# Expert layer of a four-stage kernel: blocks scatter their results to token rows, plain loads bring them back

## The reference

```
router = xf @ gate_w.T
probs = softmax(router);  top_p, top_i = top_k(probs, 2)
h = silu(xf @ expert_fc1[e].T) * (xf @ expert_fc2[e].T)      # for each expert e
out_e = h @ expert_proj[e].T
y = sum over the token's two experts of top_p * out_e
y = y + sigmoid(xf @ shared_gate_w.T) * shared(xf)
x = x + y
```

## Time and profile before

| what | value |
|---|---|
| device time, median of 3 runs (lowest to highest) | 869.14 us (868.95 to 869.23) |
| the profiled execution's own time | 869.01 us |
| its span, from the first to the last instruction | 867.2 us |
| mean granted TensorE clock (share of full speed) | 0.988 |
| PE busy, instructions | 813.6 us, 4543 matmuls |
| DVE, ACT, POOL busy | 456.9, 318.4, 161.9 us |
| transfers | 72.07 MB, mean 83 GB/s |

### The profile page before, as it was taken

The page is one execution under the profiler, slowest core; times in us unless marked ns, Lnnn a source line. Parts: engine busy times, 40 slices in busy tenths (PEclk is TensorE's granted clock), DMA queues, the critical chain, the costliest instruction groups (busy, mean ns, idle before and its releaser), DMA issues.

```text
span 867.2 us, 12754 instructions
## 1 busy us (share of the span) xinstructions
PE 813.6 (94%) x4543; PEld 568.6 (66%) x4543; DVE 456.9 (53%) x1054; ACT 318.4 (37%) x651; POOL 161.9 (19%) x256
## 2 busy tenths in 40 slices
PE   6979799889899977999999999998999999999998
PEld 3567566666567765677777776776766655555567
DVE  5999766757422225866464666476543252322223
ACT  3987777555033322443323243332312211111111
POOL 3652744113500070111111111111100000000000
PEclk9998999999999997999999999999999999999999
DMA  4002860281253230023010100100224344354431
GB/s 139 2 2 40 264 231 2 52 224 55 98 173 107 74 91 12 19 61 92 25 37 25 37 25 27 35 25 25 63 79 128 112 129 125 122 148 131 130 107 48
DMA packets 63957, 72.07 MB, mean 83 GB/s; under 512 B 14200, under 2 KB 48504, under 8 KB 63896
## 3 DMA queue, kind: packets, MB, share of 16 engines
q1 hardware_dynamic: 59048, 64.06, 24.8%
q0 software_dynamic: 1536, 4.20, 1.5%
q10 hardware_dynamic: 3312, 3.02, 1.0%
HBM read 55.45 MB, written 14.75 MB: 81 GB/s over the span
## 4 chain that ended last, share of the span: by engine, by line
PE 76%; DVE 10%; issue 5%; ACT 5%; another core or an unknown queue 1%; SPq 1%; DMA 1%; POOL 1%; DVEq 0%; ACTq 0%; POOLq 0%
PE bank L930 10%; PE bank L892 10%; PE bank L906 10%; PE bank L1107 8%; PE bank L1074 8%; PE bank L969 6%; PE bank L955 6%; PE bank L636 3%; PE bank L1857 3%; PE bank L658 2%; PE bank L1814 2%; PE bank L1841 2%; ACT arena L1914 1%; PE bank L979 1%; DVE sh L2395 1%
## 5 line engine op out<-in xcount | busy, mean ns | idle before, releaser
L1139 ACT ACTIVATE arena<-bank 128x512 f32<-128x512 f32 (+1 forms) x64 | 34.7, 544 | 230.0 <-PE bank L892 194.4
L1247 DVE TENSOR_TENSOR arena<-arena,bank 128x512 f32<-128x512 f32 (+1 forms) x47 | 30.7, 654 | 151.7 <-PE bank L906 151.7
L930 PE MATMUL bank<-arena 128*128 128x256 f32 x448 | 107.9, 382 | 1.4 <-DVE arena L1245 0.6
L892 PE MATMUL bank<-xnT,arena 128*128 128x512 f32 (+1 forms) x256 | 108.0, 544 | 0.5 <-issue 0.5
L906 PE MATMUL bank<-xnT,arena 128*128 128x512 f32 (+1 forms) x256 | 107.5, 543 | 0.0
L930 PEld LDWEIGHTS bank<-arena 128*128 128x128 f32 x448 | 85.2, 191 | 32.4 <-issue 20.6
L1208 ACT ACTIVATE arena<-bank 128x512 f32<-128x512 f32 (+1 forms) x96 | 46.8, 524 | 137.2 <-PE bank L1074 137.2
L855 POOL TENSOR_TENSOR arena<-arena,causal_t 128x256 f32<-128x256 f32 x64 | 45.0, 725 | 260.1 <-ACT arena L1213 260.1
L906 PEld LDWEIGHTS bank<-xnT,arena 128*128 128x128 f32 x256 | 49.2, 192 | 47.8 <-issue 45.9
L1107 PEld LDWEIGHTS bank<-arena 128*128 128x128 f32 x640 | 76.3, 191 | 4.4 <-POOL arena L855 2.9
L1107 PE MATMUL bank<-arena 128*128 128x129 f32 x640 | 77.0, 275 | 1.9 <-POOL arena L855 1.9
(11 more groups left out here) (236 smaller groups left out, 1173.2 us busy)
## 6 DMA issues: line engine op xcount, KB each, us to landing
arena<-in_w_gu SPq DMA_DIRECT2D x60, 256.0 KB, 3.6
rows_in<-place SPq DMA_DIRECT2D x5, 1664.0 KB, 14.2
arena<-in_w_dn SPq DMA_DIRECT2D x56, 128.0 KB, 3.6
arena<-in_wq SPq DMA_DIRECT2D x32, 128.0 KB, 2.2
arena<-in_wo SPq DMA_DIRECT2D x32, 128.0 KB, 2.0
arena<-cw_rows SPq DMA_DIRECT2D x15, 256.0 KB, 3.6
arena<-rows_in SPq DMA_DIRECT2D x23, 128.0 KB, 2.1
rows_out<-arena ACTq DMA_DIRECT2D x23, 128.0 KB, 1.7
```

The costliest lines, as they stand in the source:

```text
L892: mm = nc.tensor.matmul(ring(M)[0][:, 0:n], w_gu[:, slot_of(M), k * P:(k + 1) * P], xnT[:, k, cols], start=(k == 0), stop=(k == KD - 1))
L930: mm = nc.tensor.matmul(Y[s][half][l // 2][:, (l % 2) * DIM:(l % 2 + 1) * DIM], hh[:, M % 3, j * P:(j + 1) * P], w_dn[:, slot_of(M), :], s ...
L1139: nc.scalar.activation(sg[:, M % 2, 0:n], ring(M)[0][:, 0:n], ACT.Silu).then_inc(s_silu, 1)
```

## The change

The row that goes to an expert grows from 256 to 258 numbers. Number 256 is the token's row number in the results (written once by POOL into `xnw`), number 257 is 1 plus the expert of its first choice. POOL reads these two columns of each loaded block, works out with four small instructions where each of the 128 results belongs (first or second choice's area, row of the token; rows without a token go to places of their own) and scatters the block's result there with an indirect transfer. ACT no longer stores. SP loads the results with four plain transfers of 512 KB. `place_back` and the 16 gathers go.

```diff
-        xn = sb("xn", [P, NT, DIM])
+        xnw = sb("xn", [P, NT, DIM + 2])
+        xn = xnw[:, :, 0:DIM]
-    xg = at(14352, 768).rearrange("p (r n) -> p r n", r=3)
+    xg = at(18432, 3 * (DIM + 2)).rearrange("p (r n) -> p r n", r=3)
-    yo = at(16896, 768).rearrange("p (r n) -> p r n", r=3)
+    yo = at(16896, 1536).rearrange("p (r n) -> p r n", r=6)
...
-    rows_in = nc.dram_tensor("rows_in", ((MOE[0][0] * CAP // P + 1) * P, DIM), F32, kind="Internal").ap()
-    rows_out = nc.dram_tensor("rows_out", (NB * P, DIM), F32, kind="Internal").ap()
+    rows_in = nc.dram_tensor("rows_in", ((MOE[0][0] * CAP // P + 1) * P, DIM + 2), F32, kind="Internal").ap()
+    rows_out = nc.dram_tensor("rows_out", ((NB + 2 * NT) * P, DIM), F32, kind="Internal").ap()
...
             step(dve, nc.vector.tensor_reduce(dp.sf, dp.tk, AX.X, ALU.add))
+            step(dve, nc.vector.scalar_tensor_tensor(out=dp.gp[:, r, :, :], in0=c.lg[:], scalar=1.0,
+                                                     in1=c_exp[:].unsqueeze(1).to_broadcast([P, 4, 8]), op0=ALU.is_equal, op1=ALU.mult))
+            for b in range(2):
+                step(dve, nc.vector.tensor_reduce(xnw[:, 4 * b + 2 * r:4 * b + 2 * r + 2, DIM + 1], dp.gp[:, r, 2 * b:2 * b + 2, :],
+                                                  AX.X, ALU.add))
             nc.vector.tensor_copy(sidx[:, r, :, :], dp.sf).then_inc(s_pl, 1)
...
-        def place_back(self, dve):
...
         def block_y(self, act, j):
             act.wait_ge(s_bd, j + 1)
-            if j >= 3:
-                act.wait_ge(s_st[j % 3], 16 * (j // 3))
-            nc.scalar.copy(yo[:, j % 3, :], b_yb[:, 0:DIM]).then_inc(s_bye, 1)
-
-        def block_store(self, act, j):
-            act.wait_ge(s_bye, j + 1)
-            act.dma_start(rows_out[j * P:(j + 1) * P, :], yo[:, j % 3, :]).then_inc(s_st[j % 3], 16)
+            if j >= 6:
+                act.wait_ge(s_ro[j % 3], 16 * (j // 3 - 1))
+            nc.scalar.copy(yo[:, j % 6, :], b_yb[:, 0:DIM]).then_inc(s_bye, 1)
...
         def add_rows(self, dve, q):
-            dve.wait_ge(s_ga[min(q, 2)], 128 if q >= 2 else 64)
+            dve.wait_ge(s_ld[q // 2], 32)
...
-            zeros = attn0.zeros.unsqueeze(1).to_broadcast([P, 13, DIM])
+            flat = rows_in.rearrange("(p a) d -> p (a d)", p=P)
+            zeros = attn0.zeros[:, 0:129].unsqueeze(1).to_broadcast([P, 26, 129])
             for q in range(5):
-                sp.dma_start(rows_in.rearrange("(a p) d -> p a d", p=P)[:, 13 * q:13 * q + 13, :], zeros).then_inc(s_zf, 16)
+                sp.dma_start(flat[:, 26 * 129 * q:26 * 129 * (q + 1)].rearrange("p (a d) -> p a d", a=26), zeros).then_inc(s_zf, 16)
...
                 if j >= 3:
                     sp.wait_ge(s_bx, j - 2)
+                    sp.wait_ge(s_ix, 4 * j - 10)
...
+            for j in range(3):
+                sp.wait_ge(s_ro[j], NBL[j])
+            back = rows_out[NB * P:, :].rearrange("(k n p) d -> k p n d", k=2, p=P)
+            for q in range(2):
+                for k in range(2):
+                    sp.dma_start((xn, xg1)[k][:, 4 * q:4 * q + 4, :], back[k][:, 4 * q:4 * q + 4, :]).then_inc(s_ld[q], 16)
...
             for r in range(2):
                 pool.wait_ge(s_pl, SX[r])
...
-                                                     xn[:, l // 2 * 4 + 2 * r + l % 2, :], None).then_inc(s_rows, 16)
-            pool.wait_ge(s_tab, 3)
-            for j in range(3):
-                pool.wait_ge(s_st[j], NBL[j])
-            for n in range(NT):
-                b, r, u = n // 4, n // 2 % 2, n % 2
-                for k in range(2):
-                    nc.gpsimd.indirect_dma_start((xn, xg1)[k][:, n, :], None, rows_out,
-                                                 bass.IndirectOffsetOnAxis(ap=gidx[:, r, k, 2 * b + u:2 * b + u + 1], axis=0)
-                                                 ).then_inc(s_ga[min(n // 2, 2)], 16)
+                                                     xnw[:, l // 2 * 4 + 2 * r + l % 2, :], None).then_inc(s_rows, 16)
+            pool.wait_ge(s_tab, 2)
+            for j in range(NB + 2):
+                if j < NB:
+                    pool.wait_ge(s_cb[j % 3], 16 * (j // 3 + 1))
+                    nc.gpsimd.tensor_scalar(row_a[:, j:j + 1], xg[:, j % 3, DIM:DIM + 1], c_lane[:, j:j + 1], 0.0,
+                                            ALU.max, ALU.add).then_inc(s_ix, 1)
+                    nc.gpsimd.tensor_scalar(row_b[:, j:j + 1], xg[:, j % 3, DIM + 1:DIM + 2], dp.ej[:, j:j + 1], 1.0,
+                                            ALU.subtract, ALU.is_equal).then_inc(s_ix, 1)
+                    pool.wait_ge(s_ix, 4 * j + 2)
+                    nc.gpsimd.tensor_scalar(row_b[:, j:j + 1], row_b[:, j:j + 1], float(NT * P), row_a[:, j:j + 1],
+                                            ALU.mult, ALU.add).then_inc(s_ix, 1)
+                    pool.wait_ge(s_ix, 4 * j + 3)
+                    nc.gpsimd.tensor_copy(ridx[:, j:j + 1], row_b[:, j:j + 1]).then_inc(s_ix, 1)
+                if j >= 2:
+                    i = j - 2
+                    pool.wait_ge(s_ix, 4 * i + 4)
+                    pool.wait_ge(s_bye, i + 1)
+                    if i >= 3:
+                        pool.wait_ge(s_ro[i % 3], 16 * (i // 3))
+                    nc.gpsimd.indirect_dma_start(rows_out, bass.IndirectOffsetOnAxis(ap=ridx[:, i:i + 1], axis=0),
+                                                 yo[:, i % 6, :], None).then_inc(s_ro[i % 3], 16)
...
```

More of the change, by code:

```diff
@@ L229, in make_rest @@
     warm, spare = g["warm"], iter(range(2, 10))
-    x_sb, xn, xnT, ident, causal_t, stats, mv, std, rstd, eps_ln, rw, tri, w0 = (
-        g[n] for n in ("x_sb", "xn", "xnT", "ident", "causal_t", "stats", "mv", "std", "rstd", "eps_ln", "rw", "tri", "w0"))
+    x_sb, xn, xnw, xnT, ident, causal_t, stats, mv, std, rstd, eps_ln, rw, tri, w0 = (
+        g[n] for n in ("x_sb", "xn", "xnw", "xnT", "ident", "causal_t", "stats", "mv", "std", "rstd", "eps_ln", "rw", "tri", "w0"))
     s_xres, s_const, n_const = g["s_xres"], g["s_const"], g["n_const"]
@@ L399, in make_rest @@
     s_sy, s_cx = sem("ds_sy"), Signal(sem("ds_cx"))
-    s_ga = [sem(f"ds_ga{e}") for e in range(3)]
-    s_st = [sem(f"bl_st{j}") for j in range(3)]
+    s_ro = [sem(f"bl_ro{j}") for j in range(3)]
+    s_ld, s_ix = [sem(f"ds_ld{e}") for e in range(2)], sem("bl_ix")
     s_bx, s_bxe, s_bg, s_bsi, s_bm, s_bt, s_bte, s_bd, s_bye = (
@@ L597, in block_table @@
             nc.vector.tensor_scalar(tab[:, 1, :], dp.ej, float(E - 1), float(WE), ALU.min, ALU.mult).then_inc(s_tab, 1)
-        def place_back(self, dve):
-            E, step = MOE[0][0], self.step
-            step(dve, nc.vector.scalar_tensor_tensor(out=dp.dl, in0=dp.cb, scalar=float(P), in1=c_base[:],
-                                                     op0=ALU.mult, op1=ALU.subtract))
-            v = lambda a: a.rearrange("p r t e -> p (r t) e")
-            step(dve, nc.vector.tensor_tensor(v(dp.gp), v(dp.pos), dp.dl.unsqueeze(1).to_broadcast([P, 8, E]), ALU.add))
-            for r in range(2):
-                for k in range(2):
-                    ins = nc.vector.scalar_tensor_tensor(out=dp.tk[:, k, :, :], in0=scr[r].lg[:], scalar=float(k),
-                                                         in1=dp.gp[:, r, :, :], op0=ALU.is_equal, op1=ALU.mult)
-                    s_r.by(ins)
-                dve.wait_ge(s_r.sem, s_r.n)
-                step(dve, nc.vector.tensor_reduce(dp.gf[:, r, :, :], dp.tk, AX.X, ALU.add))
-            nc.vector.tensor_scalar(gidx[:], dp.gf, 1.0, None, ALU.subtract).then_inc(s_tab, 1)
         def block_turn(self, pe, j):
@@ L832, in pool @@
                            allow_small_or_imprecise_dtypes=True).then_inc(s_one, 1)
+            nc.gpsimd.iota(c_lane[:], [[P, NB]], base=0, channel_multiplier=1,
+                           allow_small_or_imprecise_dtypes=True).then_inc(s_one, 1)
+            nc.gpsimd.iota(xnw[:, :, DIM], [[P, NT]], base=NB * P, channel_multiplier=1,
+                           allow_small_or_imprecise_dtypes=True).then_inc(s_one, 1)
+            nc.gpsimd.iota(c_exp[:], [[1, 8]], base=1, channel_multiplier=0,
+                           allow_small_or_imprecise_dtypes=True).then_inc(s_one, 1)
+            pool.wait_ge(s_one, 7)
             pool.wait_ge(s_zf, ZF)
@@ L1045, in pe @@
             self.keys(pe, 1, b_y[0])
-            pe.wait_ge(s_one, 5)
+            pe.wait_ge(s_one, 8)
             for n in range(NH):
@@ L1291, in dve @@
                 if M == 2:
-                    dve.wait_ge(s_one, 4)
+                    dve.wait_ge(s_one, 7)
                     self.place_read(dve, 0)
@@ L1302, in dve @@
                     self.block_table(dve)
-                    self.place_back(dve)
                 if M == T0:
```

12 lines of the change are left out of this document (4 added, 8 removed).

## The result

The changed kernel took 876.25 us in the median of 7 runs (870.68 to 878.77), the kernel before 869.59 in 7 runs beside it (868.95 to 870.81). The ratio is 1.0058, 95% interval 1.0032 to 1.0084: 0.3% to 0.8% slower, where 860.9 had been forecast. The median lies 3 us above this execution, and no trace explains those 3 us.

The account below looks back on a forecast made before the run. PE was taken to bound the kernel, ending last in the chain for 76% of the span. Tail -10.7, way in +0.7 and blocks +1.8 sum to -8.2, giving 860.9 us, range 858.0 to 868.0.

Parts of the forecast that it names:

- The tail (-10.7): Behind the blocks, up to `keys(0)`: four plain loads replace 16 gathers, first stall gone, 10.7 us earlier, upper end 11.9.
- The blocks (+1.8): Load of block i + 6 waits behind POOL's scatter of block i: 0.3 us late, six rounds, +1.8, bounds 0 to 7.
- POOL's own 2.06 us a block: Among the blocks: scatter 0.96, gap 0.30 and four small instructions at 0.2 us each, under PE's 2.49.
- Rival D: Blocks: POOL becomes the bound, small instructions at 0.49 us, 3.2 us a block, giving 873.7; chance 0.09.
- The zero fill (0): Ahead of the scatters: pieces shrink from 1024 to 516 bytes, fill ends near 146 instead of 122, costing nothing.
- The way in (+0.7): Before the blocks: scatters and all block loads follow 0.7 us later.
- The three steps: In `place_rows` on DVE, ahead of the row numbers for each half: 0.7 us.
- The odd row size: Way in: rows of 1032 bytes in place of 1024 in scatters and loads, taken at nothing, upper bound 2 us.
- B: Tail: loads 3 to 6 us late or some late starts stay; gain 4.7 to 7.7, 863.9 to 866.9; chance 0.09.
- A: Blocks: load chain at its upper end, +3.5 to +7 in place of 1.8, 862.6 to 866.1; chance 0.18.
- C: Tail: late starts not from gathers, or from any indirect transfer; gain of 10.7 is nothing, 871.6; chance 0.10.

Follow-up runs that it names:

- x6: Kernel before with only the tail's edit, four plain loads (of the first 2048 result rows) instead of the sixteen gathers: 859.61 us, ratio 0.9881.
- x1: Kernel before with only the change's zero fill, 26 pieces of 516 bytes for each partition and transfer: 860.52 us against 858.18, ratio 1.0031.
- x3: Changed kernel with two small POOL index operations a block instead of four: 870.21 us, ratio 1.0148 to the kernel before.
- x11: Changed kernel with the three DVE expert-number steps moved ahead of the wait for the places: one run, 873.38 us.
- x12: Changed kernel with zero fill in wide pieces and rows of 264 numbers (1056 bytes) instead of 258 (1032 bytes): one run, 864.5 us.
- x15: Changed kernel, unchanged, as the yardstick of the fourth batch: 871.64 us, ratio 1.0018 to the kernel before.
- x14: The kernel of x12 (changed kernel, wide zero fill, rows of 1056 bytes), timed in 12 runs: 869.2 us, ratio 0.9997 to the kernel before.
- x4: Changed kernel with the four index operations of a block on DVE instead of POOL: 862.55 us, ratio 1.0058 to the kernel before.
- x9: Changed kernel with wide fill, two index operations on DVE, four buffers, early expert-number steps and spread weight loads: 859.88 us against the kernel before's 869.84, ratio 0.9879.
- x2: Changed kernel with the zero fill in 13 pieces of 1032 bytes for each partition and transfer: 868.3 us, ratio 1.0129 to the kernel before.
- x16: Kernel before, unchanged, run again for its profile in the fourth batch: 869.15 us.

## Why the prediction was wrong

The step that failed is the price of the blocks. The prediction put the chain through POOL at 1.8 us and POOL's own pace, 2.06 us a block, below PE's 2.49; POOL needs 2.89, and the blocks cost 10.3 us. A second term, the zero fill, was put at nothing and costs 2.8.

**The tail (-10.7): right, and conditional.** 10.5 us in the traces, 10.3 in x6 by times. The reading of the earlier trace rows, that the gathers and not the data delay ACT and DVE, holds: with the gathers gone the stall is gone, and the loads were hidden as costed. But the rows came from one chip. On the first batch's x1 does not have the stall, and the kernel before takes 11.6 us less there, of which the tail is 10.5. The Trainium skill ("SBUF — State Buffer", Who interferes with whom) says that PE and ACT wait for nobody at the memory ports. Here ACT starts 6.4 us later than its data allowed beside the gathers, and on time in x1 beside as many; what it waits for stays open, and so does whether it is a port.

**The blocks (+1.8): the step that failed.** It measured 10.3 us. The prediction had found the chain and its place, and priced it wrongly in each link. It took 0.27 us from the result copy to the scatter, 0.96 for it, 0.4 for two small operations and 2.84 to the turn; x3's rows have 0.75, 1.07, 0.86 and 2.97. Each is 0.1 to 0.5 us more, together 1.2. In place of 0.3 us a round it is 1.3 (8.79 less PE's 7.47). In the changed kernel POOL's own pace lies a little above this ring and sets most of them: 19 x 0.40 = 7.6 us. Of the rest, 1.5 are a longer wait and slow matmuls behind block 3 (10.29 us from turn 3 to turn 6 where it was 7.55, and the pace explains 1.2 of these 2.7), and 1.0 the ring, in two of the three late scatters (266.86 and 287.79; the third lies behind turn 22). That makes 10.1 of 10.3. The text gave 7 as the upper bound and took 1.8.

**POOL's own 2.06 us a block, "under 2.49": false.** It spends 2.89: 1.10, 0.04, 1.21, 0.54. The small operations were taken as 0.2 us, nearer a tiny write than the copies of the earlier trace rows; they took 0.18 to 0.32, with gaps 1.21 for the four. The dearer surprises were the scatter itself and the 0.54 us ahead of it, both taken from rows in which scatters followed one another (0.96 and 0.30). Rival D named this bound, at 873.7; it was given 0.09, because its price was thought to hang on the small operations alone, at 0.43 us each or more. With the scatter as it is behind computing, a mean of 0.27 us for the four sufficed for 0.40 us a block more than PE. D's mechanism is what happened, but at 7.6 us and not at its 14.6; that its 873.7 lies nearest to the measured time is luck, since the fill and the rows, which it had at nothing, made up for part.

**The zero fill (0): false.** "If pieces rule its pace it ends near 146": it ended near 160. It was costed at nothing because 66 us of other work cover it, and the fill does end before it is needed. But cover of the transfer is not cover of the engines: while the small pieces keep the DMA engines full, PE stops for "issue". x1 has 2.7 us for it. Full engines alone do not do it: the other fills have a share over 1 too (1.03 to 1.10 from 95 to 110 us) and no such stop. Whether it is the size of the pieces itself or the longer time for which they keep the engines full, no run tells apart. A packet of the instruction queue falls in 142 to 144, ahead of the stop that ends at 146.47, so I read the stops as late instruction fetches; that is argued and not shown. The Trainium skill ("Runtime: NRT & Kernel Launch", Instruction fetch mechanics) says that each engine's sequencer fetches over a DMA queue of its own and that the cost is mostly hidden. The 1.77 us stop within the full stretch would be a case where it is not.

**The way in (+0.7): the mechanism right.** The three steps cost 0.6 (x11 gives 0.5 of it back). The odd row size was taken at nothing with an upper bound of 2; it costs 0.9 (x12 gives it back).

**Rivals.** B did not come about. A was the right place at too small a price. C's time, 871.6, lies nearer than the forecast, and its reason is false on the chips where the late starts stand in the tail; on a chip without them its result, that the tail gains nothing, stands. Sum of the steps as they measured: -10.5 + 0.6 + 0.9 - 0.2 + 0.2 + 10.3 + 2.8 = 4.1.

What stays open: why the traces of some chips show the late starts and those of one do not (nor x12's), and what spreads the runs of one kernel over some 8 us on the later chips (the kernel before too: 867.1 to 874.9 in 24 runs of the second batch). The clock has a part in it: of the changed kernel's seven runs, the three longest have a mean clock of 0.984 to 0.986 and the other four 0.990 to 0.992. It is not all: x15's longest run, 874.70, has 0.992. Because of that spread x14's profile gains 6 us on x15's, and its median only 2.4.

## What to carry to other kernels

Before hiding small work on GpSimd beside a queue of indirect transfers, add up one round of that engine, with the start of a transfer behind computing and not behind another transfer; and look for rings through the in-order queues of every engine (buffers, scatter, index, load, and the turn that another block's result waits behind). When two limits lie close together, remove them in pairs, since one remedy alone may show nothing or only part (here 0 and 4 us of 10.5). A stall that no data explains may belong to the chip or the execution that was profiled: see it on a second one before a change is built on it.

## What the runs showed of the hardware

- A GpSimd operation on 128x1 numbers took 0.27 to 0.32 us (0.37 with int32 out, x3), a cast 0.18. An indirect scatter took 0.96 us with 0.30 before it in a row of scatters, 1.07 to 1.10 with 0.54 before it behind such operations, and 0.95 or 0.96 when DVE did them (x4, x9).
- Filling DRAM in pieces of 1032 bytes is slower than in pieces of 1024 or 1056. The windows from 95 to 110 us, kernel after x2 (pieces of 1032 bytes) and x12 (1056 bytes):

```profile
95.00:110.00 15.00, 11.94 (x171) 7.36 (x160) 11.43 (x37) 10.45 (x31) 13.67 (x28) 1.00 1.08 264
```

```profile
95.00:110.00 15.00, 11.99 (x165) 7.57 (x162) 11.34 (x36) 10.46 (x32) 13.39 (x27) 1.00 1.07 340
```

 In the same window the kernel before (1024 bytes) has 348 GB/s, and the changed one (516 bytes) 196, and 132 in the next. The Trainium skill ("DMA: Bandwidth & Descriptors", How a descriptor splits into AXI transactions) says that a transaction has to start at a multiple of 256 bytes, and that a descriptor which does not start at one costs extra. By that rule one row in 8 of 1056 bytes starts well and one in 32 of 1032, so seven of eight should pay; yet they are nearly as fast as rows of 1024. The sizes of 1024 and 1056 are multiples of 32 bytes, and 1032 is not; no other size was run.
- Beside runs of indirect transfers 1.26 us apart, ACT and DVE stand idle with "remote" as the releaser, for up to 12.2 us (x16), on three of the four chips of the batches and on that of the comparison. On the first batch's chip no trace has such a wait over 0.6 us, and x12's on the third has none; on the first batch's chip the same `silu` steps wait for PE, 2.2 us in the tail and 4.6 to 5.8 ahead of the blocks (x1), so only what is above that is late. Beside one scatter in 2.5 to 2.9 us no such wait behind "remote" stands in any trace.
